# A state-space layer with routed experts: two x1 tiles per block turned by DMA in place of TensorE

## What is computed

```python
xn = layernorm(x)
s = sigmoid(silu(xn @ s_w1.T + s_b1) @ s_w2.T + s_b2)      # 512 -> 256 -> 128
u = (xn @ B_w.T + B_b) * s
h[t] = h[t-1] @ A.T + u[t]                                 # over 4096 steps
y = h @ C_w.T + C_b + xn @ D_w.T + D_b
x1 = x + y * sigmoid(xn @ g_w.T + g_b)
x1n = layernorm(x1)
chosen = argmax(x1n @ gate_w.T)                            # one of 8 experts
out = x1 + x1n + x1n @ expert_w[chosen].T
```

## Time and profile before

| | us |
|---|---|
| median of 3 runs (lowest, highest) | 926.9 (925.25, 929.12) |
| the profiled execution's own time | 928.0 |
| its span, first to last instruction | 926.3 |
| TensorE busy | 904.1 |
| VectorE busy | 704.2 |
| ScalarE busy | 597.2 |
| GpSimd busy | 389.8 |

### The profile page before, as it was taken

One profiled execution on the slowest core, in us unless ns is written; L12 is line 12 of the kernel. 1 busy time (PEld: TensorE's weight loads), 2 busy tenths in 40 slices (PEclk: granted clock), 3 DMA queues, 4 the chain that ended last, 5 costly groups with the idle time before them and its releaser, 6 DMA issues.

```text
span 926.3 us, 15829 instructions
## 1 busy us (share of the span) xinstructions
PE 904.1 (98%) x4565; PEld 739.5 (80%) x4566; DVE 704.2 (76%) x1725; ACT 597.2 (64%) x826; POOL 389.8 (42%) x492
## 2 busy tenths in 40 slices
PE   8999999999999999999999999999999999999995
PEld 7777888888888888888888888888868887888884
DVE  6778979788888979788888979788787465555552
ACT  5568676857767675867767685857534345666661
POOL 1032536181634536181634527181623453333432
PEclk9999999999999999999999999999999999999998
DMA  8435384746657474748557485846789868999881
GB/s 311 131 91 140 89 206 114 205 108 171 151 140 187 89 198 120 204 111 171 153 137 186 90 199 118 206 113 178 254 275 413 336 234 243 224 218 219 192 187 39
DMA packets 203593, 165.55 MB, mean 179 GB/s; under 512 B 128245, under 2 KB 161781, under 8 KB 202496
## 3 DMA queue, kind: packets, MB, share of 16 engines
q1 hardware_dynamic: 192576, 130.89, 55.6%
q0 software_dynamic: 10800, 33.70, 10.7%
q10 hardware_dynamic: 144, 0.07, 0.0%
HBM read 81.63 MB, written 54.68 MB: 147 GB/s over the span
## 4 chain that ended last, share of the span: by engine, by line
PE 88%; DVE 3%; issue 2%; SPq 1%; ACT 1%; DMA 1%; POOL 0%; ACTq 0%; DVEq 0%; POOLq 0%
PE y L1662 19%; PE y L1382 7%; PE y L1383 7%; PE y L1384 7%; PE gates L1382 7%; PE gates L1384 6%; PE gates L1383 6%; PE scan L1527 3%; PE turned L1568 3%; PE gates L1568 3%; PE scan L1382 2%; PE scan L1383 2%; PE scan L1384 2%; PE turned L1650 2%; PE scores L1484 2%
## 5 line engine op out<-in xcount | busy, mean ns | idle before, releaser
L1662 PE MATMUL y<-experts,x1T_hi 128*128 x568 | 180.7, 399 | 2.6 <-issue 2.5
L578 POOL TENSOR_SCALAR ln_var_eps<-ln_mean_var 128x4 f32<-128x4 f32 x16 | 3.6, 224 | 302.3 <-DVE ln_mean_var L1017 302.2
L1662 PEld LDWEIGHTS y<-experts,x1T_hi 128*128 128x128 f32 x568 | 103.4, 188 | 24.1 <-issue 4.2
L623 POOL DMA_INDIRECT out<-gate,ids x71 | 72.0, 1015 | 111.1 <-DVE gate L1347 68.2
L1662 PE MATMUL y<-experts,x1T_lo 128*128 x284 | 111.4, 392 | 0.0
L1347 DVE TENSOR_TENSOR gate<-y,raw_weights 128x512 f32<-128x512 f32 x71 | 49.1, 691 | 75.6 <-PE y L1662 50.4
L1382 PE MATMUL gates<-GwT_hi,xT_hi 128*128 128x512 f32 x256 | 104.6, 409 | 0.0
L1382 PE MATMUL y<-DwT_hi,xT_hi 128*128 128x512 f32 x256 | 101.8, 398 | 0.5 <-DVE gateT L939 0.5
L731 ACT ACTIVATE joined<-flipped 128x1024 uint16<-128x1024 uint16 x60 | 82.3, 1371 | 29.7 <-DVE xT_lo L1167 21.1
L1383 PE MATMUL y<-DwT_lo,xT_hi 128*128 128x512 f32 x256 | 100.3, 392 | 0.0
L1384 PE MATMUL y<-DwT_hi,xT_lo 128*128 128x512 f32 x256 | 100.3, 392 | 0.0
(11 more groups left out here) (276 smaller groups left out, 2340.9 us busy)
## 6 DMA issues: line engine op xcount, KB each, us to landing
raw_weights<-routed_rows SPq DMA_DIRECT2D x71, 258.0 KB
x_in<-L_attn_x SPq DMA_DIRECT2D x32, 512.0 KB, 5.0
x_rows<-L_attn_x SPq DMA_DIRECT2D x32, 512.0 KB, 4.9
turned_experts<-raw_weights SPq DMA_DIRECT2D x32, 512.0 KB, 5.3
experts<-turned_experts SPq DMA_DIRECT2D x8, 2048.0 KB
raw_weights<-L_ffn_expert_w SPq DMA_DIRECT2D x32, 256.0 KB, 3.1
routed_rows<-padrow SPq DMA_DIRECT2D x9, 258.0 KB
out<-gate,ids POOLq DMA_INDIRECT x71
```

The source lines that it names most:

```text
L623: nc.gpsimd.indirect_dma_start(out=out_rows, out_offset=bass.IndirectOffsetOnAxis(ap=ids[r][:, 0:1], axis=0), in_=res[r], in_offset=None, ...
L1662: ins = nc.tensor.matmul(Y[m % 2][:], x2T[a][:, k, m % 2 * P:(m % 2 + 1) * P], flat[:, bass.ds(first + (w * KD + k) * D, D)], start=(k == ...
```

## The change

In the tails of blocks 1 to 13, which run in blocks 2 to 14, tiles 2 and 3 of x1 are not turned by TensorE. ScalarE splits each into halves, SyncE issues a DMA transpose of each ahead of those of the next input, ScalarE joins them, and the high and low parts are taken from the joined tile in SBUF. The buffer is `y_biased`, whose contents are used up by then. The score products of tiles 0 and 1 stand in TensorE's order where they stood, without the transposes between them. The other orders are changed as follows: in ScalarE's the sigmoid of gate 3 of the last block comes behind silu's first sigmoid, that of gate 1 before the copy of the second scores, and one join behind the state's copies; in VectorE's the layer-norm statistics of tile 3, the low parts of tiles 2 and 3, a gate's sum and an expert piece's low part change places; in TensorE's the second half of the scores comes after `to_middles` and is turned back after `y_dense(b, 3, 3)`. In blocks 1 to 14 the identity is added to the experts' pieces by GpSimd, behind the scatter.

The diff, cut to its core, in the order of the file (SyncE, GpSimd, ScalarE, VectorE, TensorE); the semaphores and a count are left out:

```diff
+        def by_dma(b, i):
+            return 0 < b < LASTB - 1 and i >= NT // 2
...
+        x1_halves = [yb[:, j, :].bitcast(u16) for j in range(2)]
+        x1_flipped = [yb[:, 2 + j, :].bitcast(u16).rearrange("p (c t) -> p c t", t=P) for j in range(2)]
+        x1_joined = [yb[:, j, :] for j in range(2)]
...
+                if by_dma(b - 1, NT - 1):
+                    for j in range(2):
+                        sp.wait_ge(S_["x1_halves"], 2 * (b - 2) + j + 1)
+                        sp.dma_start_transpose(x1_flipped[j], x1_halves[j]).then_inc(x1_turned[j], 16)
...
+            def add_identity(b, j):
+                f = expert_piece(b, j)[1]
+                pool.wait_ge(w_loaded[j], 16 * (b + 1))
+                part = w_raw[j][:, f * P:(f + 1) * P]
+                nc.gpsimd.tensor_tensor(part, part, ident[:], ALU.add).then_inc(w_ident[j], 1)
...
                 if b >= 2:
                     scatter(b - 2, q)
+                if 0 < b < LASTB:
+                    for j in range(2):
+                        add_identity(b + 1, j)
                 if b > 0:
                     rstd2(b - 1, 1 - q)
...
             def tail_hi(b, i):
-                act.wait_ge(S_["x2T_psum"], NT * b + i + 1)
-                nc.scalar.activation(turned_rows(b, i)[0][:, :, i % 2 * P:(i % 2 + 1) * P], by_block(turn_bank(b, i)), ACT.Copy
+                if by_dma(b, i):
+                    act.wait_ge(S_["x1_joined"], 2 * (b - 1) + i - 1)
+                    src = x1_joined[i - 2].rearrange("p (k t) -> p k t", k=KD)
+                else:
+                    act.wait_ge(S_["x2T_psum"], x1_on_pe(b, i))
+                    src = by_block(turn_bank(b, i))
+                nc.scalar.activation(turned_rows(b, i)[0][:, :, i % 2 * P:(i % 2 + 1) * P], src, ACT.Copy
                                      ).then_inc(S_["x2T_hi"], 1)
...
+            def halve_x1(b, i):
+                act.wait_ge(S_["x1_ready"], NT * b + i + 1)
+                nc.scalar.activation(x1_halves[i - 2].rearrange("p (h d) -> p h d", h=2), planes(xrow[b % 2][:, i, 0:D]), ACT.Copy
+                                     ).then_inc(S_["x1_halves"], 1)
...
+            def join_x1(b, i):
+                act.wait_ge(x1_turned[i - 2], 16 * b)
+                nc.scalar.activation(planes(x1_joined[i - 2]), x1_flipped[i - 2].rearrange("p (h k) t -> p h (k t)", h=2), ACT.Copy
+                                     ).then_inc(S_["x1_joined"], 1)
...
                 if tail:
                     high(b, NT - 1)
-                    gates(b - 1, NT - 1)
                     if b > 1:
                         halve_piece(b, 0)
...
                     wait(act, S_["silu_lo"], KH * (b - 1) + m + 1)
                     nc.scalar.activation(silu[:, m, :], (TP, G)[m][:], ACT.Sigmoid, bias=b1[:, m:m + 1]
                                          ).then_inc(S_["s1_sig"], 1)
+                    if tail and m == 0:
+                        gates(b - 1, NT - 1)
...
+                if dma:
+                    halve_x1(b - 1, 2)
+                    halve_x1(b - 1, 3)
                 if ahead:
                     halve(b + 1, 0)
                     halve(b + 1, 1)
                 else:
                     join_piece(b, 0)
                     join_piece(b, 1)
-                if tail:
+                if tail and not dma:
                     tail_hi(b - 1, 2)
                     tail_hi(b - 1, 3)
+                if tail:
                     scoresT(b - 1, 0)
-                    if ahead:
-                        join_piece(b, 0)
+                if dma:
+                    for i in range(2, NT):
+                        join_x1(b - 1, i)
+                        tail_hi(b - 1, i)
+                if tail and ahead:
+                    join_piece(b, 0)
                 if ahead:
                     join(b + 1, 0)
                 gates(b, 0)
                     high(b + 1, 0)
                     halve(b + 1, 2)
                     join(b + 1, 1)
+                if dma:
+                    gates(b, 1)
                 if tail:
                     scoresT(b - 1, 1)
-                gates(b, 1)
+                if not dma:
+                    gates(b, 1)
                 if ahead:
                     high(b + 1, 1)
                     halve(b + 1, 3)
-                    join(b + 1, 2)
+                    if not dma:
+                        join(b + 1, 2)
...
                 if ahead:
+                    if dma:
+                        join(b + 1, 2)
                     high(b + 1, 2)
                     join(b + 1, 3)
...
-                nc.vector.tensor_tensor(lo, by_block(turn_bank(b, i)), hi.bitcast(f32), ALU.subtract
+                src = x1_joined[i - 2].rearrange("p (k t) -> p k t", k=KD) if by_dma(b, i) else by_block(turn_bank(b, i))
+                nc.vector.tensor_tensor(lo, src, hi.bitcast(f32), ALU.subtract
                                         ).then_inc(S_["x2T_lo"], 1)
...
                 over(b, 0)
-                if tail:
+                if dma:
+                    ln2_stats(old, oldq, 3)
+                elif tail:
                     tail_lo(old, 2)
                 over(b, 1)
                 gate_sum(b, 0)
                 if not ahead:
                     list_tiles(0)
                 over(b, 2)
-                if tail:
+                if dma:
+                    tail_lo(old, 2)
+                elif tail:
                     tail_lo(old, 3)
-                if tail and ahead:
-                    for j in range(2):
-                        add_identity(b + 1, j)
                 over(b, 3)
-                gate_sum(b, 1)
+                if not dma:
+                    gate_sum(b, 1)
                 over(b, 4)
-                if tail and ahead:
+                if dma:
+                    gate_sum(b, 1)
+                if tail and ahead and not dma:
                     low_piece(b, 0)
                 if not ahead:
                     list_gaps()
                     slot_experts(0, FIRST)
                 over(b, 5)
-                if ahead:
+                if dma:
+                    tail_lo(old, 3)
+                elif ahead:
                     low(b + 1, 0)
                 else:
                     slot_rows(0, FIRST)
                 to_middles(b)
+                if dma:
+                    low(b + 1, 0)
                 gate_sum(b, 2)
...
                 if tail:
                     place(old, oldq, oldturn)
-                    ln2_stats(old, oldq, 3)
+                    if dma:
+                        low_piece(b, 0)
+                    else:
+                        ln2_stats(old, oldq, 3)
...
-                        wait(pe, S_["x2T_lo"], NT * b)
+                        wait(pe, S_["x2T_lo"], NT * (b - 1) + 2 if by_dma(b - 1, NT - 1) else NT * b)
...
                 y_dense(b, 1, 2, 3)
                 gates(b, 0, 0)
                 to_chunks(b)
-                if tail:
+                if tail and not by_dma(b - 1, 2):
                     tail_turn(b - 1, 1 - q, 2, True)
+                elif tail:
+                    for n in range(KD):
+                        score_product(b - 1, 0, n)
                 gates(b, 0, 1, 2)
                 over(b, 0)
-                if tail:
+                if tail and not by_dma(b - 1, 3):
                     tail_turn(b - 1, 1 - q, 3, True)
+                elif tail:
+                    for n in range(KD, 2 * KD):
+                        score_product(b - 1, 0, n)
                 gates(b, 0, 3)
                 y_dense(b, 2, 0)
                 over(b, 1)
                 gates(b, 1, 0, 1)
                 if tail:
                     tail_back(b - 1, 0)
-                gates(b, 1, 2)
-                over(b, 3)
-                gates(b, 1, 3)
-                if tail:
+                if not by_dma(b - 1, NT - 1):
+                    gates(b, 1, 2)
+                    over(b, 3)
+                    gates(b, 1, 3)
+                    if tail:
+                        tail_scores(b - 1, 1)
+                    over(b, 4)
+                    y_dense(b, 3, 0, 1)
+                    if tail:
+                        tail_back(b - 1, 1)
+                    over(b, 5)
+                    gates(b, 2, 0, 1)
+                    to_middles(b)
+                    gates(b, 2, 2, 3)
+                    y_dense(b, 3, 2)
+                    down(b)
+                    y_dense(b, 3, 3)
+                else:
+                    over(b, 3)
+                    gates(b, 1, 2, 3)
+                    over(b, 4)
+                    y_dense(b, 3, 0, 1)
+                    over(b, 5)
+                    y_dense(b, 3, 2)
+                    gates(b, 2, 0)
+                    to_middles(b)
+                    gates(b, 2, 1)
                     tail_scores(b - 1, 1)
-                over(b, 4)
-                y_dense(b, 3, 0, 1)
-                if tail:
+                    gates(b, 2, 2, 3)
+                    down(b)
```

(32 more changed lines are left out.)

## The result

The changed kernel takes 928.08 us (median of 20 runs, 925.36 to 931.15), the kernel before 926.01 in the same session (20 runs, 924.11 to 929.12): a ratio of 1.0021 with a 95% interval of 1.0011 to 1.003. It is slower by some 2 us, 0.2%, where 10.9 less was forecast. That is small, but the interval leaves out 1, and the time is above the stated range (913.5 to 926.5).

A forecast was written before the change was run, and what follows sets the result against it. TensorE's instruction stream was taken as the bound. Span 926.3 - 11.6 (removal) + 0.65 (scan's gaps) = 915.35; with 1.7 beside the span 917.05, less 1.1 for the median: 916.0 us, range 913.5 to 926.5.

The forecast's parts named there:

- The removal: TensorE, blocks 2 to 14: eight transposes fewer per block save 0.89 us each block, 11.6 us in all.
- the transposes were free: Rival: the transposes were hidden in the products' shadow on TensorE, so nothing is gained, 926.9 us; chance 0.04.
- the late landing: Rival: second x1 DMA transpose takes up to 7.7 us, making ScalarE's join and TensorE's next block late, 935.5 us; chance 0.10.
- The scan's gaps: TensorE's filler between scan steps shrinks against VectorE's answers; counted 0.05 us lost per block, 0.65 in all.
- the three tight distances: Gaps after three later scan steps, 1.60 us each against VectorE answers of 1.59, 1.50 and 1.46: no room.
- Nothing is lost, and little is left: ScalarE gets 4.65 us more per block, yet delivers the next input's high part with 0.35 us in hand.
- nothing for GpSimd: Two identity additions of 0.4 us each, behind GpSimd's last scatter where it has nothing until the next block, cost it nothing.
- the step at 375.83: Second step of the scan's level loop: filler behind it 2.30 us, no VectorE answer over 1.87, so 0.43 in hand.
- VectorE becomes the bound of the scan: Rival: three steps without room wait 0.2 us each, 0.6 a block, 7.8 in all, giving 923.8 us; chance 0.12.

The follow-up runs named there:

- e8: Changed kernel with identity additions back on VectorE, two x1 layer-norm statistics later and gate 2's sigmoid later; 918.03 us, ratio 0.9922 to the kernel before.
- e9: e8 with one quarter of a dense product of y moved in front of `over(4)`, later quarters each one place on; 925.0 us, ratio 0.9991 to the kernel before.
- e7: Changed kernel with ScalarE's sigmoid of gate 2 moved behind the last high part of the next block's input; 920.01 us, ratio 0.994 to the kernel before.
- e5: Changed kernel with GpSimd's multiplication and addition of x1 cut to 8 of 512 columns; 925.57 us against 925.37, ratio 1.000 to the kernel before.

## Why the prediction was wrong

**The removal** was right: 104 matmuls fewer, and where no one waits the distances are what the products alone take (2.07 us, forecast 2.07). Block 2, the only one without the late hand-over, takes 40.98. That the transposes were free is out. So is the late landing in the changed kernel: no wait of TensorE names one, and ScalarE waits for an x1 transpose once, 0.2 us.

**The scan's gaps** were mis-sized. I counted 0.05 us a block. Block 2 and e8 have 0.65 where 0.89 was removed, so 0.24 a block, 3.1 in all. All of it lies behind `over(2)`, where the same matmuls take 17.54 us in block 7 of e8 and 17.30 in block 8 before. 0.11 is at `over(4)`, whose two matmuls take 0.31 in place of 0.20, and 0.20 again in e9, where it has room. e9 shows 0.10 as waiting in two of the three tight distances. The rest is spread over several places and open.

**ScalarE: "Nothing is lost, and little is left"** is the step that failed. The chain was priced well for TensorE: the last high part ends at 394.88, 0.42 us ahead of the first layer, where I had 0.35, and TensorE never waits for it. Before, it ended 1.44 ahead. But TensorE isn't the only reader: VectorE takes the low part of the same tile before it turns to y and silu. It had no 0.35 in hand; it waited 0.22 us, and its whole order slid by 0.4 against TensorE (from 0.18 ahead to 0.22 behind). That left its first subtraction 0.14 later and GpSimd 0.49 earlier, enough for VectorE to fall behind GpSimd in both pairs. The two subtractions are 0.74 and 0.44 us longer than before, and z came 0.62 later. Cost: 0.61 us in each of twelve blocks, 7.3 in all; e7 gives it all back by moving one sigmoid of 0.6 us.

**GpSimd: "nothing for GpSimd"** held in its size (the additions take 0.48 us each, forecast 0.4) and failed in its place. I put them beside the answer to the step at 375.83, with 0.43 in hand. That rested on less than 0.1 us: the scatter's end at 374.82 against the end of the answer before, which the removal moves forward to 374.73 (373.31 - 0.45 + 1.87), and I did not set the two side by side. In the changed kernel the additions begin 20.94 us behind the first layer, just where the scatter ended before (20.98), but `over(0)`, held up by the silu stretch, stands at 19.64 and not at the 19.02 that my steps give (373.31 - 0.45 - 353.84), so its answer was still running. In e7, where `over(0)` is in time, the additions are 0.4 early and meet it again. The cost is 0.33 in six blocks and 0.08 in the step behind in twelve: 2.9 us by the timelines. By the Trainium skill's rule I had priced it at 4.8, beside another step's answer.

The sum: 11.6 removed, less 3.1, 7.3, 2.9 and block 7's 0.99, is 2.7 us slower over the blocks, as measured (543.95 against 541.3). Of block 7's loss one profiled execution can't tell whether it comes each time.

**The rivals.** "VectorE becomes the bound of the scan" had the engine and not the place: it priced the three tight steps, and the bulk lies in silu's stretch, which I had not looked at, since VectorE set nothing there before the change. The Trainium skill (SBUF — State Buffer, Who interferes with whom) says that a VectorE instruction with two SBUF inputs and a GpSimd instruction that reads SBUF contend, and that a cast in a two-port mode contends with GpSimd too. The traces agree in both directions, with 0.69 us alone and 1.79 contended on VectorE, and 1.30 and 1.82 on GpSimd. The cast of 0.78 us fits less well, since it began 0.2 us ahead of the addition that held it up. The prediction applied the rule to the additions that were new; it had to be applied to every pair that the change shifts.

## What to carry to other kernels

When an engine is filled until it delivers just in time for the bottleneck, look for the other readers of what it delivers, and follow their whole order from there. Where two engines' instructions hold each other up, as VectorE's and GpSimd's do here, who comes first can hang on a few hundredths of a microsecond (0.03 in block 9 of e7), and it decides which of the two grows. Keep the order in which they arrive, by moving something small out of the way. A placement "beside idle time" has to be read from the schedule after the change, since everything behind the shortened part moves too. And read the one odd block before its loss is booked to a cause: block 7's 0.99 us stands where the additions' loss stands and is not theirs.

## What was not expected of the hardware

A 128x512 subtraction on VectorE with both inputs in SBUF takes 0.69 us when GpSimd has only narrow instructions beside it. Beside a full-width one that came first it ends 0.55 us behind that one's end: in the rows above at 359.99 (359.44 + 0.55), 362.95 (361.11 + 1.30 + 0.55 = 362.96) and 402.33 (401.78 + 0.55). When VectorE is first by 0.03 us, it takes 0.69, and GpSimd's 1.30 become 1.82. In both directions the second one ends 0.14 us short of its own full length behind the first: 0.55 for 0.69, and 1.16 for 1.30 (396.75 + 1.82 - 396.72 - 0.69 in e7; 359.52 + 1.63 - 359.99 before).

A cast of 128x126 takes 0.28 us alone and 0.78 beside two GpSimd additions of 128x128, and those take 0.48 us each. Cutting nearly all of GpSimd's work on x1 (e5) did not make the kernel faster: the second x1 transpose then landed up to 8.6 us after its issue, and ScalarE waited for it.
